# Four weight residues move from VectorE to GpSimd in a macaron layer, with a new order on all engines before the attention loop

## The chip, the cores and the metric

The kernel runs on one core of a Trainium2 chip. The core has five engines with a queue of instructions each: TensorE (PE: matmuls, writes to PSUM), VectorE (DVE), ScalarE (ACT), GpSimd (POOL) and SyncE (SP, which here only issues DMAs). Each engine works through its own list in order; semaphores make one wait for another. The metric is the device time of the whole program in microseconds: 976.5 us, the median of three runs from 974.59 to 977.72.

## The reference

Three blocks follow each other on x (4 x 512 tokens of 256 values): half a mixture-of-experts feed-forward, attention, and the same feed-forward again.

```python
x = x + 0.5 * ffn(layernorm(x))
x = x + attn(layernorm(x))
x = x + 0.5 * ffn(layernorm(x))

def ffn(flat):                        # 2048 tokens, 64 experts, 4 per token, 32 slots per expert
    logits = flat @ router_w.T
    scores = softmax(logits)
    _, topk_idx = top_k(logits + router_bias, 4)
    topk_w = scores at topk_idx, divided by their sum
    # the first 32 tokens of each expert are gathered
    y = (silu(xg @ gate_w.T) * (xg @ up_w.T)) @ down_w.T
    out = scatter-add of y * weight
    # and two shared feed-forwards of width 256 run over all tokens
    return out + sum over both of (silu(flat @ sh_gate.T) * (flat @ sh_up.T)) @ sh_down.T

def attn(x):                          # 16 heads of 128, four sequences of 512 tokens
    q, k, v = x @ (codes * scales) + bias          # scales: one per 32 rows
    out = softmax(q k^T / sqrt(128)) v
    return out @ (wo_codes * wo_scales) + bo
```

## The kernel before

TensorE multiplies in 16-bit or reduced 32-bit formats, so nearly every operand is kept as two planes: a high plane (the value rounded) and a low plane (the value less its high plane), and a product is three matmuls, `high*high + high*low + low*high` (the helper `mm3`, L110 to L112). For the shared weights of the first block ScalarE writes the high plane (`job(j)`, L1037) and VectorE the low one (`low_job(j)`, L1667): j = 0 is the router's `rw`, j = 1 `gw` (gate), j = 2 `uw` (up), j = 3 `dw` (down). TensorE waits for their count `p_lo`: 1 before the router, 3 before the first gate and up product, 4 before the first down product.

The first block treats the tokens in chunks of 512, four of them (C = 0 to 3). `statistics(C)` (VectorE) and `power(C)` (GpSimd, `rstd`) and `shift(C)` (VectorE, `nmr`) give mean and scale, `normalise(C)` (ScalarE) writes `xn`, `turn(C)` transposes it on TensorE, `high(C)` and `low(C)` write the planes of `xT`. Then `router(C)`, `logits_out(C)`, `logits(C)`, and `route(C)` on VectorE, which finds the four best experts and ends with `mask`. After all four routes come `rank_keys`, `first_keys` and `indices`, from which GpSimd gathers each expert group's tokens (`gather(G)`, 16 groups of four experts). The shared feed-forward runs between: 16 pieces, each `gate_up(n)` on TensorE, `silu(n)` and `hidden_high(n)` on ScalarE, `hidden(n)` on VectorE (`hid`), `hidden_low(n)` on GpSimd (`hT`), and a `down(c)` for each four pieces. While the experts hold their PSUM banks (pieces 8 to 14), `gate_up(n)` has a single pair of banks, so each waits for the `hidden` of the piece before it.

The experts' results are scattered to `zrows` in DRAM; when all are there SyncE loads them back (`load_z(I)`, L2831), `combine(I)` adds them to x (three VectorE instructions, L1835 to L1840), and `statistics(4)` of the first attention chunk follows four combines. Attention's weights are prepared on GpSimd for each pair of heads; their scale comes from sums of squares: `squares(0)` on ScalarE (L1199 to L1203) reads the value bias `bvb` that `load_bias(0)` (L2854) brings, `norm(0)` on TensorE (L529) sums over the partitions, `scales(0)` on VectorE (L1877 to L1886) makes the power of two. Attention then runs over 64 units of a head and a sequence. From unit 8 to 55 a loop lays out each unit in a fixed order; what comes before is written out by hand, call by call, one list for each engine, and each engine keeps to its list even where the next entry waits and a later one would be ready.

Of the kernel before, what the change touches and what calls it, by code (L numbers as in the profile page):

```python
# [51 lines left out]
def f32(ap):  # L52

    return ap.bitcast(F32)
# [60 lines left out]
def macaron_layer(nc, a, out):  # L115
# [3 lines left out]
    with ExitStack() as ctx:  # L119
# [196 lines left out]
        def _(pe):  # L316
# [287 lines left out]
            turn(3)  # L604
            router(2)
            logits(1)
            gate_up(1)
            logits(2)
            router(3)
            gate_up(2)  # L610
            logits(3)
# [14 lines left out]
            turn_expert(2)  # L626
            expert_in(1)
            turn_expert(3)
            expert_hidden(0)
            expert_in(2)  # L630
            expert_out(0)
            turn_expert(4)
            expert_in(3)
            expert_hidden(1)
            turn_expert(5)
            expert_in(4)
            turn_expert(6)
            expert_hidden(2)
            expert_out(1)
            gate_up(9)  # L640
            expert_in(5)
            expert_hidden(3)
            expert_out(2)
            expert_hidden(4)
            turn_expert(7)
            expert_in(6)
            expert_out(3)
            expert_hidden(5)
            turn_expert(8)
            expert_in(7)  # L650
            expert_out(4)
            turn_expert(9)
            expert_in(8)
            expert_out(5)
            expert_hidden(6)
            turn_expert(10)
            expert_hidden(7)
            norm_qk(0)
            down(1)
            expert_hidden(8)  # L660
            expert_out(6)
            expert_in(9)
            turn_expert(11)
            expert_out(7)
            expert_in(10)
            expert_hidden(9)
            turn_expert(12)
            expert_in(11)
            expert_out(8)
            expert_in(12)  # L670
            turn_expert(13)
            expert_hidden(10)
            expert_out(9)
            expert_in(13)
            turn_expert(14)
            expert_out(10)
            turn_expert(15)
            expert_hidden(11)
            gate_up(10)
            expert_hidden(12)  # L680
            expert_hidden(13)
            expert_out(11)
            expert_in(14)
            expert_out(12)
            expert_hidden(14)
            expert_out(13)
            expert_in(15)
            expert_out(14)
            expert_hidden(15)
# [3 lines left out]
            norm(0)  # L693
            gate_up(13)
            down(2)
            gate_up(14)
            turn(4)
            gate_up(15)
            keys_of(0)
            queries(0)  # L700
            values(0)
            queries(1)
            keys_of(1)
            scores(0, 0)
            scores(0, 1)
            down(3)
            scores(0, 2)
            turn(5)
# [2410 lines left out]
```

## Time and profile before

| | us |
|---|---|
| median of three runs | 976.5 (974.59 to 977.72) |
| profiled execution, its own time | 972.94 |
| its span | 971.2 |
| PE busy | 915.0 (94%) |
| DVE busy | 763.6 (79%) |
| ACT busy | 646.6 (67%) |
| POOL busy | 645.6 (66%) |

The span runs from the first to the last instruction; the 1.7 us between it and the execution's own time lie around it. The page cuts the span into 40 slices of 24.3 us: TensorE's busy share is 9 tenths or more in most of them, and less in the first, in slices 5 and 6 (the end of the experts, before attention) and in the last four. A time in the rows below is counted in us from the span's start.

### The profile page before, as it was taken

Reading aid. Unit: us, or ns where it says so; the run is one execution under the profiler, and the core shown is the slowest. Engines: PE = TensorE matmul, PEld = TensorE weight load, DVE = VectorE, ACT = ScalarE, POOL = GpSimd, SP = SyncE. Lnnn points to the kernel's source line nnn. Section 1 sums busy time; section 2 is a strip of 40 time slices with the busy share of each in tenths; the row PEclk is TensorE's granted clock in tenths of the full one; section 3 lists DMA queues with packets and bytes.
Section 4 is the critical chain, followed back from the end, with each engine's and each line's share of the span. In section 5 each row is a group of like instructions: output and inputs, shape, how many; then the busy total and the mean of one; then the engine's idle time right before and its main releaser. Section 6 shows DMA issues by size and latency. Waiting matters only on the chain.

```text
span 971.2 us, 18502 instructions
## 1 busy us (share of the span) xinstructions
PE 915.0 (94%) x5770; PEld 561.1 (58%) x5772; DVE 763.6 (79%) x2079; ACT 646.6 (67%) x1426; POOL 645.6 (66%) x607
## 2 busy tenths in 40 slices
PE   4999789999999999999999999999999999978987
PEld 3766466555555555555555555555555555765666
DVE  6954399998888888888888888888878789876247
ACT  5634446877778687777778778777777787543431
POOL 3368778878676868778676766867677455236741
PEclk9999989999999999999999999999999999988999
DMA  8979745666765868797785766756575564485757
GB/s 338 356 247 316 270 163 163 100 136 109 153 129 101 169 151 185 141 223 158 177 192 98 153 104 137 153 103 140 107 151 96 90 120 87 89 334 153 250 204 273
DMA packets 302978, 165.58 MB, mean 170 GB/s; under 512 B 278176, under 2 KB 285600, under 8 KB 300832
## 3 DMA queue, kind: packets, MB, share of 16 engines
q1 hardware_dynamic: 297696, 146.56, 62.7%
q0 software_dynamic: 3072, 9.44, 3.0%
q10 hardware_dynamic: 2112, 8.39, 2.1%
q8 instruction: 47, 0.77, 0.3%
q14 instruction: 51, 0.42, 0.1%
HBM read 68.93 MB, written 28.31 MB: 100 GB/s over the span
## 4 chain that ended last, share of the span: by engine, by line
PE 75%; DVE 13%; DMA 4%; issue 3%; ACT 2%; SPq 1%; another core or an unknown queue 0%; POOL 0%; DVEq 0%; ACTq 0%
PE b_p L110 5%; PE b_o L110 5%; PE b_o L111 5%; PE b_o L112 5%; PE b_p L111 5%; PE b_p L112 5%; PE b_s L110 5%; PE b_s L112 5%; PE b_s L111 5%; PE b_out L110 3%; PE b_out L112 3%; PE b_out L111 3%; PE b_v L110 2%; PE b_v L112 2%; PE b_v L111 2%
## 5 line engine op out<-in xcount | busy, mean ns | idle before, releaser
L2452 POOL TENSOR_TENSOR h<-pr,h 128x512 f16<-128x512 f32 x256 | 293.1, 1158 | 160.6 <-ACT h L1171 155.1
L1161 ACT ACTIVATE pr<-b_s,nmax,kappa 128x512 f32<-128x512 f32 x256 | 197.5, 774 | 41.1 <-DVE nmax L1907 36.7
L1904 DVE TENSOR_SCALAR_CACHE_REDUCE junk<-b_s 128x512 bf16<-128x512 f32 x256 | 175.3, 685 | 22.6 <-PE b_s L112 17.5
L1171 ACT ACTIVATE h<-pr 128x512 f16<-128x512 f32 x256 | 153.3, 626 | 0.7 <-DMA pT<-h 0.4
L1935 DVE SCALAR_TENSOR_TENSOR x<-b_out,rinv,x 128x256 f32<-128x256 f32 x256 | 111.4, 476 | 41.8 <-PE b_out L112 40.3
L110 PE MATMUL b_p<-xh,w 128*128 128x512 f16 x256 | 97.8, 382 | 3.1 <-DVE qT L1846 2.2
L110 PE MATMUL b_o<-pT,v 128*128 128x512 f16 x256 | 97.1, 379 | 1.7 <-DVE oT L1923 1.7
L111 PE MATMUL b_p<-xh,w 128*128 128x512 f16 x256 | 97.8, 382 | 0.0
L110 PE MATMUL b_s<-kT,qT 128*128 128x512 f16 x256 | 97.1, 379 | 0.7 <-ACT pr L1161 0.7
L112 PE MATMUL b_p<-xh,w 128*128 128x512 f16 x256 | 97.6, 381 | 0.0
L111 PE MATMUL b_s<-kT,qT 128*128 128x512 f16 x256 | 97.1, 379 | 0.0
L111 PE MATMUL b_o<-pT,v 128*128 128x512 f16 x256 | 97.1, 379 | 0.0
L112 PE MATMUL b_s<-kT,qT 128*128 128x512 f16 x256 | 97.1, 379 | 0.0
L112 PE MATMUL b_o<-pT,v 128*128 128x512 f16 x256 | 97.1, 379 | 0.0
L2458 POOL TENSOR_TENSOR v<-vs,v 128x512 f16<-128x512 f32 x64 | 73.9, 1156 | 16.3 <-ACT v L1150 16.2
L2360 POOL TENSOR_TENSOR hT<-hid,hT 128x512 fp32r<-128x512 f32 x32 | 42.5, 1339 | 61.4 <-ACT hT L1083 61.1
L1134 ACT ACTIVATE qT<-b_p,bqs 128x512 f16<-128x512 f32 x64 | 43.9, 686 | 58.7 <-PE b_p L112 57.9
L1142 ACT ACTIVATE kT<-b_p,bks 128x512 f16<-128x512 f32 x64 | 43.9, 685 | 45.0 <-PE b_p L112 45.0
L110 PE MATMUL b_v<-w,xh 128*128 128x256 f16 x256 | 69.8, 273 | 1.5 <-issue 1.5
L110 PE MATMUL b_out<-wo,oT 128*128 128x256 f16 x256 | 70.0, 273 | 1.1 <-DVE x L1935 0.6
L112 PE MATMUL b_out<-wo,oT 128*128 128x256 f16 x256 | 69.8, 273 | 0.0
L111 PE MATMUL b_out<-wo,oT 128*128 128x256 f16 x256 | 69.8, 273 | 0.0
(223 smaller groups left out, 2234.1 us busy)
## 6 DMA issues: line engine op xcount, KB each, us to landing
raw<-in_experts SPq DMA_DIRECT2D x32, 768.0 KB, 8.0
raw_cs<-in_heads SPq DMA_DIRECT2D x16, 1024.0 KB, 5.2
zrows<-zero ACTq DMA_DIRECT2D x4, 2048.0 KB, 11.5
z<-zrows SPq DMA_DIRECT2D x16, 512.0 KB, 4.2
zrows<-zero SPq DMA_DIRECT2D x16, 512.0 KB, 3.9
zl<-zrows SPq DMA_DIRECT2D x16, 512.0 KB, 8.8
rows<-xn SPq DMA_DIRECT2D x8, 512.0 KB, 10.7
pT<-h SPq DMA_TRANSPOSE x256, 3.2
```

The costliest lines, as they stand in the source:

```text
L110: pe.matmul(out, lhs[0], rhs[0], start=first, stop=False)
L111: pe.matmul(out, lhs[0], rhs[1], start=False, stop=False)
L112: return pe.matmul(out, lhs[1], rhs[0], start=False, stop=last)
L1134: act.activation(qT[u % 2][0][:], b_p0[:], ACT.Identity, bias=bqs[:, pair_of(u) % 2, u % 2:u % 2 + 1]).then_inc(q["q_hi"], 1)
L1142: act.activation(kT[u % 2][0][:], b_p1[:], ACT.Identity, bias=bks[:, pair_of(u) % 2, u % 2:u % 2 + 1]).then_inc(q["k_hi"], 1)
L1161: act.activation(pr[n % 4][:], b_s[n % 3][:], ACT.Exp, bias=nmax[:, u % 2, i:i + 1], scale=kappa[:, s:s + 1], accum_out=rsum[:, u % 2, i:i ...
L1171: act.activation(h[n % 4][:, 0, :], pr[n % 4][:], ACT.Copy).then_inc(q["p_high"], 1)
L1904: dve.tensor_scalar(junk[n % 2][:], b_s[n % 3][:], 0.0, None, ALU.add, ALU.max, accum_out=peaks[:, n % 2:n % 2 + 1]).then_inc(q["peak_read ...
L1935: ins = dve.scalar_tensor_tensor(out=xs, in0=b_out[:, t * D:(t + 1) * D], scalar=rinv[:, u % 4, i:i + 1], in1=xs, op0=ALU.mult, op1=ALU.add)
L2360: pool.tensor_tensor(hT[1][:, n % SM, :], hid[n % 2][:], f32(hT[0][:, n % SM, :]), ALU.subtract).then_inc(q["hlo_done"], 1)
L2452: pool.tensor_tensor(h[n % 4][:, 1, :], pr[n % 4][:], h[n % 4][:, 0, :], ALU.subtract).then_inc(q["p_split"], 1)
L2458: pool.tensor_tensor(lo, vs[half][:].rearrange("p t f -> p (t f)"), hi, ALU.subtract).then_inc(q["v_lo"], 1)
```

## The change: what it does

GpSimd computes the four low planes in place of VectorE, with the same instruction (`tensor_tensor` with `subtract`) on the same tiles. No other instruction is added or removed. All five written-out lists up to attention's twelfth unit or so get a new order. The diff is cut to what the prediction speaks of:

```diff
@@ block.vector
-            def low_job(j):
-                src, (hi, lo), sem = shared[j]
-                dve.wait_ge(q["p_hi"], j + 1)
-                dve.tensor_tensor(lo, src[:], f32(hi), ALU.subtract).then_inc(q["p_lo"], 1)
@@ block.gpsimd
+            def low_job(j):
+                src, (hi, lo), sem = shared[j]
+                pool.wait_ge(q["p_hi"], j + 1)
+                pool.tensor_tensor(lo, src[:], f32(hi), ALU.subtract).then_inc(q["p_lo"], 1)
...
-            power(0)
             identity()
             selectors()
-            countdown()
+            low_job(0)
+            power(0)
             power(1)
             power(2)
+            low_job(1)
             power(3)
+            low_job(2)
+            countdown()
+            earlier()
+            scale_weights(0, 0)
+            low_job(3)
             hidden_low(0)
...
@@ block.scalar
             job(0)
+            job(1)
             normalise(0)
-            job(1)
             high(0)
+            job(2)
             normalise(1)
             logits_out(0)
-            job(2)
             normalise(2)
+            normalise(3)
             high(1)
...
@@ block.vector
             fills()
             statistics(0)
+            pads()
             shift(0)
+            statistics(1)
+            statistics(2)
             picks()
-            statistics(1)
-            pads()
-            statistics(2)
+            low(0)
             shift(1)
-            low(0)
-            low_job(0)
-            low_job(1)
+            shift(2)
             statistics(3)
-            shift(2)
             shift(3)
-            low_job(2)
+            route(0)
             low(1)
-            route(0)
             low(2)
-            low_job(3)
             low(3)
             route(1)
             hidden(0)
+            hidden(1)
             route(2)
-            hidden(1)
             route(3)
...
@@ block.tensor
             gate_up(12)
             norm(0)
+            down(2)
             gate_up(13)
-            down(2)
             gate_up(14)
             turn(4)
...
@@ block.sync
-            load_bias(0)
-            load_bias(1)
             load(14)
             load(15)
             load_vo(0)
             load_z(0)
+            load_bias(0)
             load_z(1)
```

The order in which the instructions then stand is shown at three places. A line number after the change is a few less than before it.

GpSimd, its start, before: `rstd` is `power`, `down_t` is `countdown`, `rank_f` belongs to `earlier`, `hT` is `hidden_low`.

```order
L2350 TENSOR_TENSOR rstd<-veps,mhalf 128x4
L2485 MEMSET ident 128x128
L2486 AFFINE_SELECT ident<-ident 128x128
L2504 IOTA dump 128x16
L2505 MEMSET selj 64x64
L2506 AFFINE_SELECT selj<-selj 64x64
L2499 IOTA down_t 64x1024 x2
L2350 TENSOR_TENSOR rstd<-veps,mhalf 128x4 x3
L2360 TENSOR_TENSOR hT_110<-hid_107,hT_109 128x512
```

The same stretch after the change, from the first three `rstd` on. The low plane of `rw` stands right ahead of them, and the first `hT` right behind the last row; `gw`, `uw` and `dw` are `low_job(1)` to `low_job(3)`.

```order
L2341 TENSOR_TENSOR rstd<-veps,mhalf 128x4 x3
L2346 TENSOR_TENSOR gw<-raw_g,gw 128x1024
L2341 TENSOR_TENSOR rstd<-veps,mhalf 128x4
L2346 TENSOR_TENSOR uw<-raw_u,uw 128x1024
L2495 IOTA down_t 64x1024 x2
L2506 MEMSET rank_f 128x128
L2507 AFFINE_SELECT rank_f<-rank_f 128x128
L2509 AFFINE_SELECT rank_f<-rank_f 128x128
L2511 MEMSET rank_f 64x64
L2512 CAST rank_w<-rank_f 128x128
L2406 TENSOR_TENSOR raw_cs<-raw_cs 128x512
L2346 TENSOR_TENSOR dw<-raw_d,dw 128x1024
```

What stood in GpSimd's first row is now behind the router's plane, `uw` follows directly on the last `rstd`, and `dw` stands ahead of the first `hT`.

SyncE between the last expert weights and the results loaded back, before: `bvb_60` is `load_bias(0)`, `raw_cs` attention's weights, `z` the results.

```order
L2790 DMA raw_76<-in_experts 128x1536
L2854 DMA bvb_60<-in_bv 128x256
L2854 DMA bvb_61<-in_bv 128x256
L2790 DMA raw_70<-in_experts 128x1536
L2790 DMA raw_71<-in_experts 128x1536
L2846 DMA raw_cs<-in_heads 128x2048
L2831 DMA z_80<-zrows 128x1024
L2831 DMA z_81<-zrows 128x1024
```

The same stretch after the change:

```order
L2790 DMA raw_70<-in_experts 128x1536
L2790 DMA raw_71<-in_experts 128x1536
L2846 DMA raw_cs<-in_heads 128x2048
L2831 DMA z_80<-zrows 128x1024
L2854 DMA bvb_60<-in_bv 128x256
L2831 DMA z_81<-zrows 128x1024
```

The first value bias is now issued behind the first load of results, which waits for the last scatter; the second one, further on.

VectorE where the combines begin, before: `z` and `x<-x,z` are `combine`, `hid` is `hidden`, `bound` the first instruction of `scales(0)`.

```order
L1750 TENSOR_TENSOR hid_107<-up,sil_105 128x512
L1750 TENSOR_TENSOR hid_108<-up,sil_106 128x512
L1835 TENSOR_TENSOR z_80<-z_80 128x512
L1837 TENSOR_TENSOR z_80<-z_80 128x256
L1840 TENSOR_TENSOR x<-x,z_80 128x256
L1750 TENSOR_TENSOR hid_107<-up,sil_105 128x512
L1877 TENSOR_REDUCE bound<-b_p 128x2
```

After the change:

```order
L1745 TENSOR_TENSOR hid_107<-up,sil_105 128x512
L1745 TENSOR_TENSOR hid_108<-up,sil_106 128x512
L1754 SCALAR_TENSOR_TENSOR x<-tb,x 128x512 x2
L1830 TENSOR_TENSOR z_80<-z_80 128x512
L1832 TENSOR_TENSOR z_80<-z_80 128x256
L1835 TENSOR_TENSOR x<-x,z_80 128x256
L1872 TENSOR_REDUCE bound<-b_p 128x2
```

Piece 12's `hid` has gone from ahead of `bound` to behind the second combine, and the addition of the second down product (`x<-tb,x`) has come in ahead of the first combine.

## Rows read from the trace of the kernel before

**Rows 1.** Stretches: length, then PE, PEld, DVE, ACT, POOL busy; clock, DMA share, GB/s
```profile
15.60:43.00 27.40, 25.73 (x128) 21.03 (x128) 24.35 (x92) 17.30 (x30) 4.96 (x9) 1.00 0.97 384
...
66.00:112.00 46.00, 40.51 (x512) 25.02 (x511) 16.33 (x63) 24.04 (x80) 36.21 (x38) 1.00 0.79 277
112.00:147.00 35.00, 26.92 (x138) 20.93 (x136) 28.82 (x47) 13.23 (x32) 26.43 (x23) 0.90 0.51 184
147.00:241.00 94.00, 89.69 (x522) 52.39 (x523) 83.86 (x221) 72.98 (x153) 78.36 (x79) 0.98 0.61 128
241.00:251.10 10.10, 10.10 (x61) 5.64 (x60) 9.24 (x24) 7.11 (x15) 5.99 (x6) 1.00 0.98 208
```

**Rows 2.** DMA issues over the whole run: KB each, us from issue to landing
```profile
raw_u<-in_sh_up_w SPq DMA_DIRECT2D x1, 512.0 KB, 7.2
raw_g<-in_sh_gate_w SPq DMA_DIRECT2D x1, 512.0 KB, 8.8
```

**Rows 3.** ScalarE timeline, 8 to 17 us: start, duration, instruction, idle before
```profile
7.75 2.08 ACT L1055 ACTIVATE xn<-x,nmr,rstd 128x256 f32<-128x256 f32 x4 [1.51 <-DVE nmr L1695]
12.43 1.06 ACT L1037 ACTIVATE gw<-raw_g 128x1024 fp32r<-128x1024 f32 x1 [2.60 <-DMA raw_g<-in_sh_gate_w]
```

**Rows 4.** TensorE timeline, 8 to 15.9 us
```profile
9.88 1.97 PE L338 MATMUL tb<-ident,xn 128*128 128x128 f32 x8 [9.88 <-ACT xn L1055]
15.63 0.77 PE L351 MATMUL rl<-xT,rw 128*128 128x512 f32 x1 [3.78 <-DVE rw L1667]
```

**Rows 5.** VectorE timeline, low plane of gw, route 1 and the masks of routes 1 and 2
```profile
15.40 1.22 DVE L1667 TENSOR_TENSOR gw<-raw_g,gw 128x1024 fp32r<-128x1024 f32 x1
...
30.30 0.42 DVE L1728 TENSOR_TENSOR lgb<-rl,rbias 128x256 f32<-128x256 f32 x1 [0.19 <-PE rl L360]
...
33.14 0.42 DVE L1741 TENSOR_TENSOR mask<-lgb,lgr 128x256 f32<-128x256 f32 x1
...
36.91 1.29 DVE L1741 TENSOR_TENSOR mask<-lgb,lgr 128x256 f32<-128x256 f32 x1
...
41.90 1.38 DVE L1750 TENSOR_TENSOR hid<-up,sil 128x512 f32<-128x512 f32 x2
```

**Rows 6.** GpSimd timeline, start
```profile
18.64 1.01 POOL L2350 TENSOR_TENSOR rstd<-veps,mhalf 128x4 f32<-128x4 f32 x1 [4.28 <-DVE veps L1688]
36.64 1.28 POOL L2360 TENSOR_TENSOR hT<-hid,hT 128x512 fp32r<-128x512 f32 x1 [17.00 <-ACT hT L1083]
...
49.43 2.41 POOL L2366 TENSOR_TENSOR ex<-ex,mask 128x1024 f32<-128x1024 f32 x1
```

**Rows 7.** GpSimd timeline, 170 to 178 us
```profile
173.13 1.26 POOL L2400 TENSOR_TENSOR z<-z 128x512 f32<-128x512 f32 x1
```

**Rows 8.** VectorE timeline, 170 to 178 us
```profile
173.25 1.17 DVE L1695 SCALAR_TENSOR_TENSOR nmr<-mv,rstd 128x4 f32<-128x4 f32 x1
```

**Rows 9.** SyncE timeline, 114 to 117 us
```profile
114.04 1.75 SPq L2831 DMA_DIRECT2D z<-zrows  x4
```

**Rows 10.** The tile bvb over the whole run, its loads
```profile
DMA to landing us min/median/max: 4.9/5.8/7.1
```

**Rows 11.** ScalarE timeline, 113 to 120 us
```profile
116.27 0.63 ACT L1199 ACTIVATE square<-raw_cs 128x512 bf16<-128x512 f32 x1 [1.95 <-POOL raw_cs L2410]
...
117.30 0.61 ACT L1203 ACTIVATE square_qk<-raw_cs 128x512 bf16<-128x512 f32 x1
```

**Rows 12.** VectorE timeline, 117 to 137 us
```profile
117.56 0.69 DVE L1835 TENSOR_TENSOR z<-z 128x512 f32<-128x512 f32 x1 [2.52 <-DMA z<-zrows]
...
119.69 0.15 DVE L1877 TENSOR_REDUCE bound<-b_p 128x2 f32<-128x4 f32 x1
...
121.40 0.69 DVE L1835 TENSOR_TENSOR z<-z 128x512 f32<-128x512 f32 x1
...
129.42 1.41 DVE L1682 BATCH_NORM_STATS2 stats<-x 128x6 f32<-128x256 f32 x4
```

**Rows 13.** TensorE timeline, 128 to 133 us
```profile
132.10 0.79 PE L110 MATMUL gate<-xT,gw 128*128 128x512 f32 x1 [3.77 <-DVE hid L1750]
```

More of the change, by code:

```diff
@@ L781, in _ @@
             probs_values(4, 2)
+            norm(1)
+            output(3, 0)
             probs_values(4, 3)
-            scores(6, 3)
-            output(3, 1)
             keys_of(8)
             scores(7, 0)
+            values(7)
             queries(8)
+            output(3, 1)
             probs_values(5, 0)
@@ L2044, in _ @@
             combine(7)
+            maxima(0, 0)
             statistics(5)
-            maxima(0, 0)
+            queries(1)
+            values(0)
+            shift(5)
             maxima(0, 1)
+            maxima(0, 2)
             keys_of(1)
-            queries(1)
-            shift(5)
-            values(0)
             add_shared(3)
-            maxima(0, 2)
             low(5)
@@ L2099, in _ @@
             values(5)
-            add(1, 1)
+            add(1, 0)
             maxima(5, 0)
+            maxima(5, 1)
             outputs(2)
             sums(3)
-            maxima(5, 1)
+            add(1, 1)
+            queries(6)
             keys_of(6)
             maxima(5, 2)
-            values(6)
-            queries(6)
             add(2, 0)
+            maxima(5, 3)
             sums(4)
-            scales(1)
-            maxima(5, 3)
-            add(2, 1)
             outputs(3)
@@ L2116, in _ @@
             maxima(6, 1)
-            add(3, 0)
+            values(6)
+            add(2, 1)
+            maxima(6, 2)
             keys_of(7)
             queries(7)
+            maxima(6, 3)
+            scales(1)
+            add(3, 0)
             outputs(4)
-            maxima(6, 2)
-            maxima(6, 3)
+            values(7)
             maxima(7, 0)
@@ L2604, in _ @@
             probs_low(0, 2)
-            power(6)
             values(0)
             probs_low(0, 3)
+            combine(13)
+            power(6)
+            values(1)
             probs_low(1, 0)
-            values(1)
             probs_low(1, 1)
-            combine(13)
             combine(14)
+            combine(15)
             probs_low(1, 2)
@@ L2659, in _ @@
             probs_low(7, 3)
+            range_weights(1, 3)
             high_weights(1, 3)
+            values(8)
             low_weights(1, 3)
-            values(8)
             for u in range(8, 56):
@@ L2898, in _ @@
             load(3)
-            load(4)
             store_rows(0)
@@ L2902, in _ @@
             store_rows(2)
+            load_down()
+            load_qk_bias()
             load_qk(0)
+            load(4)
             store_rows(3)
@@ L2930, in _ @@
             load_z(9)
+            load_bias(1)
             load_z(10)
```

507 lines of the change are left out of this document (248 added, 259 removed).

## Prediction

> **What bounds the kernel now.** I read the busy time by stretch first. In the attention loop TensorE has no idle time at all: 10.10 of 10.10 us from 241.0 on [rows 1]. The loop's code is the same, so a new order before it is worth just as much as it moves the loop's start. Before the loop TensorE is idle for 1.7 us in 15.6 to 43, 5.5 in 66 to 112, 8.1 in 112 to 147 and 4.3 in 147 to 241 (length less PE busy) [rows 1]. All the matmuls stay, so what can be won or lost is this idle time, that of the start, and the work done at the lower clock level: the granted clock averages 0.90 in 112 to 147 [rows 1].
>
> Second, the timelines of the start, to see who holds TensorE up. Its first transposes run from 9.88, then it stands still for 3.78 us until the low plane of the router's weights is there, and starts the router at 15.63 [rows 4]. That plane waited for VectorE, which waited for the high planes of xT, which ScalarE started only after `gw`, and `gw` waited for its DMA until 12.43 [rows 3]. From 30.3 to 43.3 VectorE works without a gap: routes 1 to 3 and four `hid` [rows 5]. It is busy 24.35 of 27.4 us there [rows 1].
>
> Third, the end of the experts. The first results land 2.52 us late for VectorE at 117.56 and from there it works its list through: combines, the scales of the value weights from 119.69 to 121.4, statistics from 129.42 [rows 12]. TensorE waits 3.77 us for the `hid` behind those statistics and goes on at 132.10 [rows 13]. So from 117 to about 147 the order on VectorE sets the pace, and each microsecond that it loses there reaches the loop.
>
> **The change, part by part.** Each price is against the profiled execution.
>
> *Low planes off VectorE.* Three instructions of 1.22 us [rows 5] and a small one leave it, some 3.9 us. On GpSimd a 128x1024 product of two SBUF tiles took 2.41 us and a 128x512 subtraction of the same form 1.28, twice that 2.56 [rows 6]; I take 2.5 each. GpSimd idled 17.0 us there before its first `hT` [rows 6], so its own time is free.
>
> *The first chunk.* ScalarE's `gw` copy now stands ahead of the first `xn`. Its load is now fifth in the DMA list, where `raw_u` stood; that one, issued at 2.65, landed 7.2 us later, at 9.85 [rows 2]. So: `gw` 9.85 to 10.9 (1.06), `xn` to 13.0 (2.08) [rows 3], transposes to 14.95 (1.97) [rows 4], high and low plane of the second half about 1.3, router at 16.3: 0.7 later than 15.63. The wait on `rw` that ended TensorE's 3.78 us goes, but the late `xn` takes its place.
>
> *Chunks 1 to 3.* `uw`'s plane follows on the last `rstd` in GpSimd's list with nothing between. Elsewhere in this trace a `nmr` of four values per partition took 1.17 us beside a GpSimd addition that began 0.12 us ahead of it [rows 7, 8]; both ended together. So I expect the last `nmr` to stand behind `uw` for about 2.5 us, and `normalise(3)` with it, which ScalarE now has ahead of `high(1)`. That delays chunk 1's planes by some 3 us, but `route(0)` has been pulled ahead of them and fills that time. By the durations route 1 starts at 30.8 to 31.3 in place of 30.30 [rows 5]: +0.7.
>
> *The masks.* Route 2's `mask` took 1.29 us, against 0.42 for route 1's, beside an `hT` from 36.64 to 37.92 [rows 5, 6]. In its place now stands `dw`'s plane, twice as long, waiting for the `dw` copy that ScalarE makes only after the last `lgT`, about 37 to 38. If the mask falls at its start it loses 1.9 us in place of 0.87; somewhere in it, half of that. I take +0.8 (bounds -0.9, when it falls in no GpSimd instruction, and +1.6). The start in all: +1.5 us, bounds -2 and +3.5.
>
> The Trainium skill ("SBUF — State Buffer", section "Who interferes with whom") says that a VectorE instruction with two SBUF inputs contends with a GpSimd instruction that reads SBUF, and that whoever is first keeps the shared port for the whole instruction. The trace agrees: 1.17 us [rows 8] and 1.29 us [rows 5]. It speaks against moving such work to GpSimd; by it each of the three 2.5 us planes can hold VectorE up, which is the third rival below.
>
> *Experts, 66 to 112.* 5.5 us of idle time in many small pieces [rows 1]. The new list turns tokens earlier, takes the addition of the second down product off VectorE's list here, and puts ScalarE's weight squares ahead of the experts. I take -1.0, bounds -2.5 and +1.5.
>
> *The value bias.* `load_bias(0)` is now issued behind `load_z(0)`, and that one waits for all scatters: it was issued at 114.04, four such issues taking 1.75 us [rows 9]. So the bias is issued at 114.5 and lands 5.8 us later, at 120.3 (bounds 4.9 and 7.1) [rows 10]. `squares(0)` waits for it. It started at 116.27 and ended at 117.91 [rows 11], 1.64 us; now it ends at 121.9. Then comes TensorE's `norm(0)`, 0.4 us, and VectorE's scales, which started at 119.69 [rows 12], start at 122.4: 2.7 us later, with VectorE idle, since no other entry of its list may pass. ScalarE's `silu(12)` is behind `squares(0)`, and `down(2)` behind `norm(0)`. Besides, piece 12's `hid` (0.6) now lies behind the scales, before the statistics. Together +3.3 us on the chain of VectorE, bounds +2.4 (landing in 4.9) and +4.6 (in 7.1). Nothing covers it: the 2.52 us wait [rows 12] lies ahead of it and goes to the addition of the second down product.
>
> *After the statistics.* `shift(4)` has slipped behind a combine, so `xn` comes some 3 us later, but TensorE is in `gate_up(14)` meanwhile; +0.3, bounds 0 and +3. In 147 to 241 the 4.3 us of idle time [rows 1] come from small waits; a new order takes or adds some: -0.5, bounds -3 and +3.
>
> Sum: 1.5 - 1.0 + 3.3 + 0.3 - 0.5 = +3.6 us. The profiled execution had 972.94, so 976.5 on its own footing. It lay 3.6 below the median of 976.5, so the median after is 976.5 + 3.6 = 980.1; I say 980.
>
> **The rivals.** 0.3% is 2.9 us, about what a measurement here can tell from no change.
>
> *No change.* The bias lands late as I say, but the stretches around give it back: the experts at their bound of -2.5, the start even. For it: all these are idle pieces that a new list can pack. Time: 3.3 - 2.5 = +0.8, so 977.3. Chance 0.32.
>
> *Faster.* The freed VectorE time counts. Place: 15.6 to 43, where VectorE is 89% busy [rows 1]. If the planes of xT and the routes close up by what left, 3.9 us, and `gw`'s earlier landing lets the router start before 15.63, the experts begin 4 us sooner; then with -1.0 and +3.3 it is -1.6, and with the experts and attention at better halves of their bounds (-1.5 each) -4.6: 971.9. It decides itself at route 1: the rival needs its start before 28. Against it: of the four planes only the first two stood directly ahead of something that TensorE waited for. Chance 0.20.
>
> *Port conflicts dominate.* The three GpSimd planes each hold up a `nmr`, a `veps` or a mask for their full 2.5 us: 7.5 us less the 0.9 paid before, of which the last two are on the chain: +4.1 in place of +1.5 at the start. Then 976.5 + 3.6 + 2.6 = 982.7. For it rows 7 and 8, against it that most of VectorE's instructions in the routes ran beside `hT` at their usual length. Chance 0.13.
>
> My forecast has 0.35, and with the port rival slower has 0.48. Faster 0.20, same 0.32, slower 0.48. The range for 8 in 10 goes from 972 (the faster rival) to 986 (half of each upper bound used: 980 + 1.0 for the start, 0.7 for the bias, 1.3 for the experts and 3 for what follows the statistics); the forecast's own is 978 to 983.
>
> **What would show it.** Right: in the profile after, the `square` of L1199 released by the DMA of `bvb`, near 120 or 5.8 us after the first `z` issue; VectorE idle for some 3 us ahead of `bound`; TensorE waiting for it ahead of the second half of the down products; a `nmr` or a `mask` above 1 us at the start, beside `uw` or `dw`; the router's first matmul near 16.3. Wrong: a `bvb` that lands within 2 us, a route 1 before 28 us, or a loop that starts later or earlier than the sum of these steps, which would put the cause in 147 to 241. TensorE at the lower clock level for longer than in the 0.90 stretch would add to it without being in my sum.

## The result, and the profile after

The changed kernel took 982.37 us (median of 6 runs, 980.97 to 983.97) against 976.27 for the kernel before on the same chip (6 runs, 973.39 to 977.72): ratio 1.0068, interval 1.0049 to 1.0087. It is slower by 6.6 us by the ratio and 6.1 by the medians; 980.0 was forecast, in a range from 972 to 986. The profiled execution took 983.88 us (span 982.2), 10.9 more than that of before: it lay 1.5 us above its median, and that of before 3.3 below. So 4.8 us of the difference between the two profiles are not in the medians, and where in the table below they lie is not known.

Where the two profiles part, by the starts of the same instructions:

| start of | before | after | difference |
|---|---|---|---|
| first transposes | 9.88 | 13.21 | +3.3 |
| router(0) on TensorE | 15.63 | 16.59 | +1.0 |
| route(1) | 30.30 | 32.84 | +2.5 |
| first gather | 61.67 | 65.12 | +3.5 |
| last expert output on ScalarE | 110.76 | 118.38 | +7.6 |
| first `z` on VectorE | 117.56 | 125.04 | +7.5 |
| `bound` (scales of the value weights) | 119.69 | 130.18 | +10.5 |
| scores(0, 0) | 152.08 | 162.09 | +10.0 |
| first matmul of the loop (unit 8) | 240.71 | 250.21 | +9.5 |

Three steps: the start, the experts, the value bias. After them the new order gives back 1.0 us in this profile. These are the stretches of [rows 1] in the profile after; they are the same times, but as all work lies later, not the same work (length; PE, PEld, DVE, ACT, POOL busy; granted clock, DMA share, GB/s):

```profile
15.60:43.00 27.40, 23.24 (x111) 18.99 (x112) 23.29 (x75) 17.55 (x31) 14.08 (x14) 1.00 0.96 350
66.00:112.00 46.00, 40.25 (x449) 25.51 (x447) 14.28 (x56) 19.89 (x67) 33.38 (x36) 0.93 0.75 258
112.00:147.00 35.00, 26.06 (x176) 19.52 (x168) 21.75 (x39) 10.29 (x28) 24.00 (x24) 0.90 0.58 208
147.00:241.00 94.00, 87.98 (x504) 53.57 (x505) 82.14 (x215) 73.84 (x158) 75.72 (x73) 0.96 0.63 136
241.00:251.10 10.10, 10.10 (x67) 6.29 (x65) 8.43 (x22) 6.97 (x16) 8.68 (x10) 1.00 0.40 75
```

From 15.6 to 43 GpSimd has 9 us more to do, and VectorE, which gave up three planes of 1.22 us, is busy only 1.1 us less. Its timeline shows why (against [rows 5] and [rows 8]):

```profile
7.59 1.41 DVE L1677 BATCH_NORM_STATS2 stats<-x 128x6 f32<-128x256 f32 x4 [5.00 <-DMA x<-in_x]
...
16.45 1.98 DVE L1690 SCALAR_TENSOR_TENSOR nmr<-mv,rstd 128x4 f32<-128x4 f32 x2
...
21.49 2.34 DVE L1690 SCALAR_TENSOR_TENSOR nmr<-mv,rstd 128x4 f32<-128x4 f32 x1 [1.12 <-POOL rstd L2341]
...
32.84 0.41 DVE L1723 TENSOR_TENSOR lgb<-rl,rbias 128x256 f32<-128x256 f32 x1
...
40.24 2.09 DVE L1736 TENSOR_TENSOR mask<-lgb,lgr 128x256 f32<-128x256 f32 x1
```

The GpSimd timeline beside it:

```profile
15.94 2.40 POOL L2346 TENSOR_TENSOR gw<-raw_g,gw 128x1024 fp32r<-128x1024 f32 x1
...
21.42 2.39 POOL L2346 TENSOR_TENSOR uw<-raw_u,uw 128x1024 fp32r<-128x1024 f32 x1
...
39.61 2.43 POOL L2346 TENSOR_TENSOR dw<-raw_d,dw 128x1024 fp32r<-128x1024 f32 x1 [5.64 <-ACT dw L1037]
```

Each of the three planes holds one small VectorE instruction until it ends: `gw` ends at 18.34 and the pair of `nmr` at 18.43, `uw` at 23.81 and the third `nmr` at 23.83, `dw` at 42.04 and the mask at 42.33. A `nmr` has four values per partition. Alone it takes 0.16 us, and the mask 0.42. Below I call this a hold. An `xT`, which reads one operand from PSUM, was not held: at 15.85 it takes its usual 0.69 us beside `gw`'s plane.

The value bias came as forecast. ScalarE first, then VectorE (answers to [rows 11] and [rows 12]), then TensorE's first transposes for attention and its first scores:

```profile
127.77 0.63 ACT L1199 ACTIVATE square<-raw_cs 128x512 bf16<-128x512 f32 x1 [4.42 <-DMA bvb<-in_bv]
```

```profile
130.18 0.16 DVE L1872 TENSOR_REDUCE bound<-b_p 128x2 f32<-128x4 f32 x1 [2.36 <-PE b_p L529]
...
139.34 1.41 DVE L1677 BATCH_NORM_STATS2 stats<-x 128x6 f32<-128x256 f32 x4
```

```profile
150.51 1.97 PE L338 MATMUL b_p<-ident,axn 128*128 128x128 f32 x8 [4.74 <-ACT axn L1055]
162.09 0.38 PE L110 MATMUL b_s<-kT,qT 128*128 128x512 f16 x1
```

VectorE's `nmr` for these transposes, behind `combine(4)` now, lasts 1.22 us in place of 0.16, until GpSimd's `raw_cs` ends at 148.33:

```profile
147.13 1.22 DVE L1690 SCALAR_TENSOR_TENSOR nmr<-mv,rstd 128x4 f32<-128x4 f32 x1
```

### The profile page after: what moved, and what is told of

The parts are those of the page before. It is cut to its first block, busy times and chain, and to the rows that moved or that the text cites. A ratio compares the mean times of both kernels' runs of the same rounds, so it can differ in the third digit from the quotient of the medians.

```text
span 982.2 us, 18501 instructions
## 1 busy us (share of the span) xinstructions
PE 919.3 (94%) x5770; PEld 565.6 (58%) x5772; DVE 761.1 (77%) x2075; ACT 646.9 (66%) x1426; POOL 652.4 (66%) x611
## 4 chain that ended last, share of the span: by engine, by line
PE 79%; DVE 8%; DMA 5%; issue 3%; ACT 3%; POOL 1%; SPq 1%; another core or an unknown queue 0%; DVEq 0%; ACTq 0%; POOLq 0%
PE b_o L110 5%; PE b_o L111 5%; PE b_o L112 5%; PE b_p L110 5%; PE b_p L112 5%; PE b_p L111 5%; PE b_s L110 5%; PE b_s L111 5%; PE b_s L112 5%; PE b_out L110 3%; PE b_out L112 3%; PE b_out L111 3%; PE b_v L110 3%; PE b_v L112 3%; PE b_v L111 3%
## 5 line engine op out<-in xcount | busy, mean ns | idle before, releaser
L110 PE MATMUL b_out<-wo,oT 128*128 128x256 f16 x256 | 70.0, 273 | 0.8 <-DVE x L1930 0.4
L112 PE MATMUL b_v<-w,xh 128*128 128x256 f16 x256 | 69.8, 273 | 0.0
L112 PE MATMUL b_out<-wo,oT 128*128 128x256 f16 x256 | 69.8, 273 | 0.0
L111 PE MATMUL b_v<-w,xh 128*128 128x256 f16 x256 | 69.8, 273 | 0.0
```

The lines of the kernel that those rows point to most:

```text
L110: pe.matmul(out, lhs[0], rhs[0], start=first, stop=False)
L111: pe.matmul(out, lhs[0], rhs[1], start=False, stop=False)
L112: return pe.matmul(out, lhs[1], rhs[0], start=False, stop=last)
```

## The experiments

Besides the two kernels of the result, twelve were timed, on four other chips. The chips differ. On three (the one of the result and two of these) the kernel before takes 974 to 976 us: **kind A**. On the other two it takes 1001 to 1002: **kind B**. All ratios are to the kernel before on the same chip. Experiments 1, 2, 3 and 5 ran on one chip of kind B, and 4, 6, 7 and 9 on the other; the changed kernel ran on the second only.

| kernel | kind | median, us | ratio to before, interval |
|---|---|---|---|
| after | A | 982.37 | 1.0068 (1.0049 to 1.0087) |
| after again | B | 999.78 | 0.9977 (0.9950 to 1.0004) |
| after, bias early | B | 997.00 | 0.9946 (0.9924 to 0.9969) |
| after, shift(4) early | B | 998.61 | 0.9971 (0.9950 to 0.9992) |
| after, x loaded first | B | 998.38 | 0.9970 (0.9948 to 0.9993) |
| after, low planes on VectorE | B | 998.19 | 0.9963 (0.9943 to 0.9982) |
| before, low planes on GpSimd | B | 1000.43 | 0.9984 (0.9963 to 1.0005) |
| after's order to the first gather, then before's | B | 1005.29 | 1.0030 (1.0002 to 1.0058) |
| the same | A | 980.73 | 1.0058 (1.0043 to 1.0073) |
| before's order to the first gather, then after's | B | 997.03 | 0.9952 (0.9931 to 0.9974) |
| after's experts alone | A | 976.36 | 1.0027 (1.0014 to 1.0039) |
| before's start; after's experts and prelude, both repaired | A | 974.37 | 1.0005 (0.9990 to 1.0020) |
| before through the experts; after's prelude, repaired | A | 970.26 | 0.9962 (0.9948 to 0.9976) |

("Prelude" is what lies between the last expert output and the loop; "repaired" is with the bias load and shift(4) where before had them.)

The kinds were not known when the first four expectations were written; absolute times in them are meant for the chip of the result.

**1. The bias load alone (kind B).** Edit of the changed kernel, in SyncE's list:

```diff
             load(13)
+            load_bias(0)
             load(14)
...
             load_z(0)
-            load_bias(0)
```

> The changed kernel with one edit: the load of the first value bias is back ahead of the last two expert weights in SyncE's list, so that it lands before it is wanted. Theory (the late bias stops TensorE's norm and VectorE's scales): in the profile after, VectorE idled 2.36 us ahead of `bound` and TensorE 3.7 us ahead of `norm(0)`; both go, and as nothing else covers VectorE's chain there the time falls by 2.4 to 3.5 us, to about 979.4. Rival (the wait is slack that another wait takes over, such as the loads of the results or `silu(12)`): less than 1 us, 982.

The VectorE timeline, with no wait left ahead of `bound`:

```profile
133.30 1.48 DVE L1830 TENSOR_TENSOR z<-z 128x512 f32<-128x512 f32 x1
...
135.61 0.15 DVE L1872 TENSOR_REDUCE bound<-b_p 128x2 f32<-128x4 f32 x1
```

From the first `z` to `bound` it is 2.3 us, against 4.4 to 4.9 in the five other kernels on kind B that have the late load, and from the first `z` to the loop 120.6 against 122.8 in the changed kernel. The late load costs 2.1 to 2.6 us there, and 3.0 in the profile of the result (5.14 from `z` to `bound` against 2.13 before). Of the time, the edit gives 3.1 us by the ratios (0.9946 against 0.9977), in the range of the theory; but the changed kernel was timed on the other chip of kind B, and the two intervals overlap. The kernels of experiments 2 and 3, which keep the late load, ran on this chip and are 1.6 and 1.4 us slower. So the sign is well supported, and the size of the time rests on the profiles.

**2. shift(4) alone (kind B).** In VectorE's list:

```diff
             hidden(13)
+            shift(4)
             combine(4)
-            shift(4)
             combine(5)
```

> The changed kernel with one edit: on VectorE `shift(4)` stands ahead of `combine(4)` again. Theory (my price of +0.3 us for this step was too small: TensorE waited 4.7 us for `axn` ahead of `turn(4)`, and `combine(4)` with the blocked `nmr` behind it took 4.6 us): the time falls by 3 to 4 us, to about 979. Rival (the combine only moves behind it and holds up the low plane of `turn(4)`, so the first projection starts as late as now): less than 1 us, 982.

TensorE in this kernel, then in the changed one on a chip of the same kind:

```profile
154.07 1.09 PE L338 MATMUL b_p<-ident,axn 128*128 128x128 f32 x8 [0.88 <-ACT axn L1055]
...
160.51 0.38 PE L110 MATMUL b_p<-xh,w 128*128 128x512 f16 x1 [2.55 <-DVE xh L1699]
...
167.60 0.38 PE L110 MATMUL b_s<-kT,qT 128*128 128x512 f16 x1
```

```profile
157.05 1.09 PE L338 MATMUL b_p<-ident,axn 128*128 128x128 f32 x8 [2.17 <-ACT axn L1055]
...
167.52 0.38 PE L110 MATMUL b_s<-kT,qT 128*128 128x512 f16 x1
```

The transposes come 3 us earlier and TensorE then waits 2.55 us for VectorE's `xh`; the first scores start at the same time. The wait only changed its place: VectorE's list is the limit there. The difference of the two ratios, 0.0006, is within both intervals, so on kind B the rival holds and the 3 to 4 us of the theory do not.

On kind A the edit alone was not run, and the profiles speak for a loss there. From `bound` to the first scores it is 31.91 us in the profile of the result, and 29.09 to 29.33 in the two kernels here. The kernel of experiment 11 (kind A) has the changed order there except for shift(4), which is ahead of its combine, and takes 29.40. So up to 2.5 us of the result's profile may be this step. It is one profile against one.

**3. x ahead of the router's loads (kind B).** In SyncE's list, with VectorE's first statistics as the thing to watch:

```diff
-            load_router()
             load_x(0)
             load_x(1)
+            load_router()
```

> The changed kernel with one edit: SyncE loads the first two chunks of x ahead of the router's weights and bias. In the profile after, the first statistics began at 7.59 in place of 4.37. Theory A (the copy of `gw`, which lands at 10.1 and stands ahead of the first `xn` on ScalarE, sets the start, so the late x costs nothing): statistics at 4.4, first transposes still near 13, time lower by 0 to 0.5 us: 982. Theory B (the 3.2 us pass through to the end, by the later statistics of chunks 1 and 2): 979.2.

```profile
4.35 1.40 DVE L1677 BATCH_NORM_STATS2 stats<-x 128x6 f32<-128x256 f32 x4 [1.76 <-DMA x<-in_x]
```

The statistics start at 4.35 again and not at 7.69 to 8.34, where the other kernels on kind B with the late x have them, but the first transposes stay at 13.21 and the router at 16.59, to the hundredth as in the profile of the result: there ScalarE's `gw` copy, which waits for its own load until 10.1, stands ahead of `xn`. Route 1 is 1.5 us earlier (31.31 in place of 32.84; the two other kernels of this chip have 33.17 and 32.69). So of the 2.5 us at route 1 the late x carries about 1.5. Part of that is a hold: `gw`'s plane now begins at 14.49, and the pair of `nmr` behind it takes 0.52 us in place of 1.98. The time, 0.9970 against 0.9977 for the changed kernel on the other chip, cannot tell theory A from theory B.

**4 and 5. Who computes the low planes (kind B).** The changed kernel with the four planes back on VectorE:

> The changed kernel with the four low planes back on VectorE, at the places where before's order has them, all else as in the change. Theory P (port: each GpSimd plane holds a small VectorE operation for about 1 us, and the last two holds are on the path to the routing): VectorE takes up 4 planes of 1.2 us of which two lie in idle time, the three holds of 1 us go: route 1 and the first gather within 0.7 us of the changed kernel's. Rival D (the GpSimd planes cost nothing on the path; the start is late only for the later x): VectorE's 2.5 us of planes ahead of the second routing come on top, and route 1 and the first gather are 2 to 2.5 us later than in the changed kernel.

```diff
@@ block.vector (of the changed kernel)
             low(0)
+            low_job(0)
             shift(1)
             shift(2)
+            low_job(1)
             statistics(3)
             shift(3)
+            low_job(2)
             route(0)
...
             route(2)
+            low_job(3)
```

The two `nmr` and the mask of route 2 on VectorE's timeline:

```profile
17.03 0.23 DVE L1695 SCALAR_TENSOR_TENSOR nmr<-mv,rstd 128x4 f32<-128x4 f32 x2
...
21.45 0.16 DVE L1695 SCALAR_TENSOR_TENSOR nmr<-mv,rstd 128x4 f32<-128x4 f32 x1 [1.12 <-POOL rstd L2350]
```

```profile
38.72 0.43 DVE L1741 TENSOR_TENSOR mask<-lgb,lgr 128x256 f32<-128x256 f32 x1
```

All three holds are gone, and although VectorE does the planes again, route 1 starts at 31.32 (33.99 in the changed kernel on the same chip) and the first gather at 63.26 (66.23): 3.0 us earlier. Five other profiles with the three holds and the late x, on either kind, have their first gather at 64.96 to 65.46, so 1.7 to 3.0 us is the fair range. Both expectations were wrong, P too, which had the two even: a plane costs its engine 1.22 us once, while a hold of 1.7 to 2.2 us falls on whatever is next, which was ScalarE's `xn` twice and the rest of the routes once. At the end of the program the medians differ by 1.6 us, with overlapping intervals, so how much of it is left there is not shown. The other way round, before's order with the planes on GpSimd:

> The kernel before with the four low planes alone moved to GpSimd, at the first places where their inputs are ready; all five lists keep the old order otherwise. Theory (the shared port: a `nmr` or `mask` of VectorE stands still while GpSimd writes a plane of 2.4 us): a `nmr` or a mask of over 1 us in the trace and a time 0 to 3 us above the 976.3 of before. Rival (the 3.9 us freed on VectorE count, as it is 89% busy there): route 1 starts 2 to 4 us earlier than 30.30 and the time falls to 973.

```diff
@@ block.gpsimd (of the kernel before)
             countdown()
             power(1)
+            low_job(0)
             power(2)
+            low_job(1)
             power(3)
+            low_job(2)
+            low_job(3)
             hidden_low(0)
```

Here `uw`'s plane runs from 19.53, after the last `nmr` at 18.80, and holds nothing up; the keys come at 45.11, against 44.63 in a kernel with before's start on the other chip of kind B. `gw`'s plane, from 14.75 to 17.15, stands directly behind a `rstd` as in the change, but VectorE has `xT` and statistics to do meanwhile, at their usual lengths, and comes to its `nmr` at 17.58. The one mask above 1 us is route 2's, 1.31 us beside an `hT`, as in before. The time is that of the kernel before (0.9984, interval to 1.0005). So neither side was right: no new hold, and route 1 at 31.44, not 2 to 4 us earlier. What hurts is not the engine but the moment: in the change each plane is under way when VectorE comes to an instruction with both operands in SBUF, a `nmr` twice and a mask once.

**6. The changed kernel again, on a chip of kind B.**

> The changed kernel itself, again, beside the kernel before on the chip that the next three run on. Theory A (the change costs the same few us on every chip, as the sum of my terms has it): 3 to 7 us slower than the kernel before, ratio 1.003 to 1.007. Theory B (the experts stage depends on the chip: where the gathers land late, the order of before loses more in it than that of after, as 56.7 us against 64.4 us in that stage hints): within 0.3% of the kernel before or up to 0.4% faster where the kernel before takes about 1001 us, and 3 to 7 us slower where it takes about 976 us.

0.9977: not slower there. The time is as theory B has it, and theory A, one cost on every chip, falls. A row of waits tells the kinds apart (us in total, times, longest, whole run):

```profile
ACT xgT L1108 <- remote: 6.8, 3, 3.3
...
ACT y L1127 <- remote: 3.6, 3, 1.7
ACT esil L1114 <- remote: 2.6, 1, 2.6
DVE ehid L1820 <- remote: 2.4, 1, 2.4
```

"remote" is a release that the profile finds no instruction of this core for. All eight kernels that were profiled on kind B have 11 to 20 us of such waits on ScalarE, all in the two expert stages; on kind A no kernel has any on ScalarE, before's own profile included. The sum, 13.0 us on ScalarE in this run, is most of the 17.4 us that the changed kernel takes longer on kind B, if all of it is on the path, which is not shown. What the engine waits for is not shown either. From the first turned tokens to the last expert output the changed kernel takes 56.7 us on kind B and 48.9 on kind A; before's order 57.7 and 64.4 in the two kernels that have it on B (experiments 7 and 5), and 45.1 on A. The 64.4, on which theory B was built, come from an execution 6.1 us above the median of its kernel (1006.5 us against 1000.43), with 20.0 us of such waits on ScalarE. So what theory B says of that stage is not shown.

**7 and 8. The start alone, on both kinds.**

> After's order only up to the first gather (its low planes on GpSimd with it), from there on the order of before. The start alone. Theory S (the later start, first gather +3.5 us in the trace of after, is passed on whole to the end of the first block): 3.0 to 4.0 us slower than the kernel before. Rival T (the experts stage absorbs it, because its transfers are its limit): under 1 us slower. Trace: the first turned gather at 69 to 70 us against 66 to 67 of before's order in either; the last expert output moves with it by S, and does not by T.

> After's order up to the first gather alone, once more, on the chip that this call gets. Where the kernel before takes about 1002 us it was 3.3 us slower than it. Theory (the start's delay of 3.5 us is passed on whole on every chip): 3 to 4 us slower again. Rival (the start shifts the experts stage against its weight loads, so that its worth depends on the chip): outside of that, down to 0 or up to 6 us.

Slower by 3.0 us by the ratio on kind B (interval 0.2 to 5.8) and 5.7 on kind A (4.2 to 7.1). So on A the start is passed on, even more than the 3 to 4 us of the theory; on B the interval holds both S and its rival T. But the joint has a fault of its own: before's order has the load of attention's output bias `bo` (128 KB) early, after's late, and in the joined list it is issued at 60.78, right ahead of the gathers. TensorE's first turn of gathered tokens:

```profile
71.60 0.69 PE L450 MATMUL gate<-ident,xg 128*128 128x128 f32 x2 [2.49 <-DMA xg<-rows,tok_i]
```

That is 6.3 us behind the first gather (65.27), against 4.3 in the profile after (65.12 and 69.45). Less these 2.0 us the start is worth some 3.7 us on kind A. This is an estimate from the two gaps, not a measurement. Nor is the gap all: against the kernel of experiment 12 on the same chip, which has before's start and before's experts, the first gather is 3.5 us later, the first turned tokens 5.9, and the last expert output 7.9. After its wait of 2.49 us TensorE ran at the lower clock level:

```profile
72.00:78.00 6.00, 5.30 (x57) 2.92 (x55) 1.54 (x7) 2.39 (x7) 3.58 (x4) 0.50 0.39 113
```

**9. The rest alone (kind B): before's start, after's order from the first gather on.**

> Before's order and its low planes on VectorE up to the first gather, from there on after's order: everything else of the change. Sum of the terms: bias load +3.0, shift of unit 4 +2 to +3, loop prelude -0.5, experts stage -1.0 to +0.5 at an equal clock: 3.5 to 6 us slower than the kernel before where it takes 976 us. Rival (the whole loss of the change is its start): within 1 us of the kernel before. Where the kernel before takes 1001 us the experts stage of after was 7.7 us shorter than that of before, and the sum is then -2 to -4 us.

0.9952: 4.8 us faster by the ratio, more than the 2 to 4 of the sum, and far from the rival's 1. With the start's +3.0 it adds up to -1.8; the changed kernel on the same chip has -2.3. Of this kernel's 4.8 us the prelude, by experiment 12 less the late bias, is worth 3.7 - 2.3 = 1.4, if it is worth the same on both kinds. The other 3.4 would be after's experts stage, which loses on kind A (next). The profiles do not bear that out: from the first gather to the last expert output it is 63.3 us here, 60.8 to 62.2 in the five other kernels with after's experts stage on kind B, and 64.1 in experiment 7, which has before's experts and 2.0 us of the joint's fault in it. Why the order is not slower on kind B is open; the stage alone was not run there.

**10 and 11. The experts, and the best of the pieces (kind A).**

> After's order from the first gather to the last expert output alone; start, combining and loop prelude as before, with both value biases loaded just ahead of the first load of gathered sums. Theory E (the order of the experts stage is the one part of the change whose worth depends on the chip): where the kernel before takes about 1002 us, that stage took 56.7 us in after's order and 64.4 in before's, of which the slower chip is to give back 5 to 8 us: ratio 0.992 to 0.995; where it takes about 976 us, within 1 us. Rival F (the gain of h_rest lies in the prelude of the loop, not in the experts): within 1 us of the kernel before on either. Trace: the last expert output lies 5 us or more ahead of that of before's order by E.

> Before's order up to the first gather, after's order from there on, with the first value bias loaded ahead of expert group 14 and unit 4's shift ahead of its combine: the three losses that I name taken out of the change, its experts stage and its loop prelude kept. Theory (the terms add): where the kernel before takes about 1002 us, after's later part gave 5.0 us, the bias is worth 2.3 to 2.8 and the shift about 1.2: 8 to 9 us faster than the kernel before, ratio 0.991 to 0.992. Where the kernel before takes about 976 us, the experts stage gives nothing at an equal clock and the prelude -0.5: within 1.5 us of the kernel before. Rival (bias and shift cover one wait, so that only the larger counts): 7.5 us faster on the first kind of chip, 1 to 2 us slower on the other.

After's experts stage alone costs 2.3 us on kind A (1.0027); "within 1 us" was wrong. What theory E says of the slower chips could not be seen here. The stretches in which it happens, in the kernel before, the changed kernel and this one (columns as above, the clock is the third from the right):

```profile
72.00:78.00 6.00, 5.17 (x50) 3.35 (x42) 3.79 (x13) 3.95 (x18) 5.12 (x5) 1.00 0.83 255
78.00:84.00 6.00, 5.86 (x102) 3.08 (x105) 1.95 (x9) 3.45 (x13) 4.99 (x5) 1.00 0.90 303
```

```profile
72.00:78.00 6.00, 3.19 (x46) 1.61 (x46) 3.69 (x12) 3.19 (x11) 4.90 (x6) 0.98 0.42 117
78.00:84.00 6.00, 5.45 (x47) 3.25 (x48) 2.64 (x11) 1.25 (x5) 3.91 (x4) 0.50 0.71 236
```

```profile
72.00:78.00 6.00, 3.86 (x49) 2.11 (x45) 4.26 (x14) 1.68 (x6) 4.02 (x4) 0.67 0.63 218
78.00:84.00 6.00, 6.00 (x45) 3.80 (x45) 0.86 (x4) 1.41 (x5) 2.98 (x4) 0.76 0.57 184
```

In after's order TensorE is idle for 2.8 of the 6 us from 72, and then the granted clock is 0.50, the level of 1.2 GHz, through 78 to 84. In before's order a shared product (`gate_up(9)`) fills that place and the clock stays at 1.00. Over 66 to 112 the granted clock is 1.00 in before and in the kernel of experiment 12, and 0.89 to 0.93 in the four others on kind A. In the profile after the idle time begins on VectorE:

```profile
74.81 1.67 DVE L1811 TENSOR_TENSOR wtmp<-xg,sel 128x64 f32<-128x64 f32 x1
...
78.12 0.28 DVE L1820 TENSOR_TENSOR ehid<-rl,esil 128x128 f32<-128x128 f32 x1
```

A `wtmp`, 0.22 us elsewhere, lasts until GpSimd's `hT` (75.11 to 76.38) ends; three more pairs of slot weights stand ahead of the `ehid` that TensorE waits 1.95 us for. A `wtmp` of 1.9 us that ends with an `hT` is in these two kernels too (71.44 and 71.50). So it looks like a hold again, in a place where neither order had a low plane, but it began 0.30 to 0.54 us ahead of the `hT`, which a hold by `hT` alone does not explain. I had no kernel in which only this is taken out; that it brings about the idle time and with it the clock is read off the timelines, not tested. The best-of-pieces kernel speaks against it as the only cause: there TensorE is at 0.50 through 72 to 78 already, and its wait for that `ehid`, 0.84 us, ends at 75.20.

The best-of-pieces kernel stands even with before (1.0005). That is within the 1.5 us expected, but by luck: the sum had the experts at nothing and the prelude at -0.5, and by experiment 12 they are +4.1 and -3.7.

**12. The prelude alone (kind A).**

> Before's order through the last expert output, then after's order into the loop, with unit 4's shift ahead of its combine and the value biases where before's order has them. Theory (terms add): h_best, with after's experts stage, stood 0.3 us above the kernel before and h_exp 2.3 us, so the prelude alone gives -2.0 us: 1.5 to 2.5 us faster than the kernel before, ratio 0.9975 to 0.9985, on either kind of chip. Rival (the prelude only pays behind after's experts stage, because its shared products were laid out for it): within 0.5 us of the kernel before, or slower. If the theory holds this is the one piece of the change that beats both kernels where the kernel before takes about 975 us.

970.26 us, 0.9962 (0.9948 to 0.9976): by the ratio 3.7 us faster than the kernel before and the only piece that beats both on kind A. The rival falls, and the gain is larger than the 1.5 to 2.5 that the sum gave. The other repaired kernel differs from this one by after's experts stage, which so costs 4.1 us (974.37 less 970.26, two chips of kind A). TensorE in this kernel and in that of before:

```profile
142.30 0.59 PE L110 MATMUL b_p<-xh,w 128*128 128x512 f16 x1 [2.10 <-DVE xh L1704]
...
147.78 0.38 PE L110 MATMUL b_p<-xh,w 128*128 128x512 f16 x1
...
149.08 0.38 PE L110 MATMUL b_s<-kT,qT 128*128 128x512 f16 x1
```

```profile
141.50 0.39 PE L110 MATMUL b_p<-xh,w 128*128 128x512 f16 x1
...
147.81 0.38 PE L110 MATMUL b_p<-xh,w 128*128 128x512 f16 x1 [2.23 <-DVE qT L1846]
...
152.08 0.38 PE L110 MATMUL b_s<-kT,qT 128*128 128x512 f16 x1
```

Before has keys_of(1), 12 matmuls, and a wait of 2.23 us ahead of the first scores; after has the scores first. From the first projection to the first scores it is 6.8 us in place of 10.6, and the loop starts at 236.74 in place of 240.71.

## Why the prediction was right, and where it was not

The sign came out and the time lies within the range; of the size little more than half was forecast: +3.6 us against +6.1 measured. The mechanism that carried the forecast, the late value bias, is confirmed. That the sum is as near as it is, is luck: the start is 2 us and the experts are 3.3 to 5.1 us too low in it, and the prelude stands 3.2 us too high against them. On kind B, of which the prediction knew nothing, the same change is not slower.

- **The value bias, +3.3:** right. +3.0 in the profile, 2.1 to 2.6 on kind B. The load landed 5.6 us after its issue (5.8 taken) and VectorE was idle for 2.36 us ahead of `bound`, TensorE for 3.71 ahead of `norm(0)`.
- **The start, +1.5:** too small, though inside its upper bound of 3.5; +3.5 at the first gather. The first chunk came as forecast (router 16.3, measured 16.59). Two things were mis-sized. First, the late x: no term of the sum has it. It was issued 0.9 us later and landed 3.2 us later, about 1.5 of which reach route 1 (experiment 3). Second, the holds: I priced the one behind `uw` as covered by route(0) and the mask at +0.8. Both happened at full length, and a third at `gw`; together the holds cost 1.7 to 3.0 us at the first gather (experiment 4), and they overlap with the late x. The rival "port conflicts dominate" put the start at +4.1 and the time at 982.7; of the cases that I weighed it describes the start best and, with the luck above, the time too. I gave it 0.13.
- **The experts, -1.0:** wrong, in sign on this chip, and beyond its bound of +1.5. It is +3.9 in the profile, +2.3 alone and +4.1 by the difference of two kernels. I read the idle pieces that a new list can pack, and not what a new list can open: the gap at 75, and the lower clock level behind it, which the prediction named as outside its sum. A loop that starts later than the sum, by 9.5 us in place of 3.6 in the profile, was among its signs of being wrong; it would have put the cause in 147 to 241, but the surplus lies in the start and here. What opens the gap is read, not tested.
- **After the statistics, +0.3:** right on kind B, where moving shift(4) back moves the wait and gains nothing (experiment 2). On kind A it was not tested, and is probably too small: TensorE waited 4.74 us for `axn` in the profile of the result, and the way from `bound` to the first scores took 2.5 us more than in a kernel with shift(4) moved back.
- **The prelude of attention, -0.5:** the step that failed on the other side. I counted only 147 to 241 (88.63 us from the first scores to the loop before, 88.12 after: -0.5 indeed) and overlooked that TensorE's list brings the first scores ahead of keys_of(1). That is worth 3.0 us by the first scores of experiment 12, and with the rest of the prelude 3.7 us of time, with shift(4) and the bias repaired. In the profile of the result only 1.0 us of it is seen between `bound` and the loop.

Summed from kernels on kind A, with the bias as in the profile: 3.7 for the start, 2.3 to 4.1 for the experts, 3.0 for the bias, -3.7 for the prelude, so 5.3 to 7.1, against 6.1 to 6.6 measured. That it fits is no proof of each term: the start's is an estimate, the bias is from profiles, and shift(4) is left out, which could add up to 2.5. Open are the cause of the waits called "remote" and so why a chip is of one kind or the other, why the changed order is not slower on kind B, what opens the gap among the experts, what shift(4) costs on kind A, and what the start alone costs without the fault of the joint.

## What to carry to other kernels

Work moved to GpSimd is not priced by how idle GpSimd is, but by the VectorE instruction with two SBUF operands that comes right behind its start, however small (here 2.34 us in place of 0.16). Put it where VectorE reads an operand from PSUM (`xT` kept its 0.69 us beside a plane) or waits anyway, and check every such pair on the timelines. A change of order is a sum of pieces with signs of their own: split it at points where both orders have issued the same calls, and keep the pieces that win (here one of four on kind A). And where chips differ, as here by 2.7% for one kernel, a verdict holds for the chip that it was measured on: the same edit was 0.7% slower on one kind and not slower on the other.

## What the runs showed of the hardware that I had not expected

Two small loads at the head of the queue, 64 KB of router weights and the router's bias, 32 KB spread over all partitions, nearly stop what follows. DMA throughput in steps of 0.3 us from 0 to 12 us in the kernel before, and in the changed one with the two loads (KB, us to landing):

```profile
GB/s 0 0 0 0 0 0 205 41 137 328 396 423 396 437 410 410 352 197 131 11 30 83 128 226 265 305 373 412 423 423 437 437 382 410 423 437 423 423 396 423
```

```profile
GB/s 0 0 0 0 0 0 183 44 22 58 26 36 69 12 193 265 261 359 301 369 382 410 410 410 423 437 410 437 423 437 410 423 410 396 423 423 410 423 410 498
...
raw_r<-in_router_w SPq DMA_DIRECT2D x1, 64.0 KB, 1.8
rbias<-in_router_bias SPq DMA_DIRECT2D x1, 32.0 KB, 4.7
```

In the changed kernel the rate stays between 12 and 69 GB/s for 2.1 us ahead of x; in that of before the hole lies behind the first x. It cost x 3.2 us of landing for 0.9 us of later issue. In seven profiles with these loads first the statistics start at 7.6 to 8.3 us, in seven with x first at 4.4 to 4.5. Experiment 3, which moves both back, shows that it is these two; the 64 KB land in 1.8 us and the 32 KB in 4.7, which points at the bias, but neither was moved alone.

The second surprise is what holds cost: an instruction of four values per partition took 2.34 us instead of 0.16, and three holds cost more on the path than the planes do on VectorE (first gather at 64.96 to 66.23 against 63.26). The third is the clock: after waits of 1.95 and 2.49 us TensorE ran 6 us at a granted 0.50 in two kernels, the changed one and that of experiment 8. The fourth are the two kinds of chip, with 11 to 20 us of waits on ScalarE on one that the other does not have.
